# Where the bias tiles of the next region stand among the steps of a region: ten of thirteen behind column tiles, three behind row tiles

## What is computed

```python
rel  = tril(t - s)
nd   = log(|c * rel| + 1) / (log(|c * pos| + 1) + EPS)
h    = relu(nd[..., None] * W1[0] + b1)
bias = einsum('qkm,mh->qkh', h, W2) + b2
y    = x + bias
```

```python
ret = einsum('MTS,MN->NTS', y, w + eye)
ret = ret + sum_i einsum('ITS,TIM->MTS', einsum('MTS,TIM->ITS', y, qw1), qw2) + y * qdd
ret = ret + sum_i einsum('ITS,SIM->MTS', einsum('MTS,SIM->ITS', y, kw1), kw2) + y * kdd
```

## Time and profile before

| what | value |
|---|---|
| time, median of 3 runs | 895.82 us (891.65 to 903.48) |
| the profiled execution's own time | 896.75 us |
| its span, first to last instruction | 894.9 us |
| mean granted TensorE clock | 0.894 of full speed |
| busy share: PE / DVE / ACT / POOL | 78% / 54% / 44% / 57% |
| DMA packets | 148.98 MB, 166 GB/s over the span |

### The profile page before, as it was taken

One profiled execution on the slowest core, in us unless ns is written; L12 is line 12 of the kernel. 1 busy time (PEld: TensorE's weight loads), 2 busy tenths in 40 slices (PEclk: granted clock), 3 DMA queues, 4 the chain that ended last, 5 costly groups with the idle time before them and its releaser, 6 DMA issues. The chain is left out here.

```text
span 894.9 us, 28881 instructions
## 1 busy us (share of the span) xinstructions
PE 699.0 (78%) x12836; PEld 586.1 (65%) x12836; DVE 481.0 (54%) x629; ACT 395.8 (44%) x428; POOL 513.4 (57%) x463
## 2 busy tenths in 40 slices
PE   0466767986998798696699859969988896699764
PEld 0254566875887688585577657756866685589664
DVE  7667625863693595475346625653475365335412
ACT  5756536544743663563245325433543453232000
POOL 4524823734475257368558937985898588635300
PEclk9876978988998899899899979998999999799857
DMA  6578559597778979877885888589859897843905
GB/s 129 137 169 147 132 145 205 128 227 169 181 185 208 208 149 223 213 159 150 189 195 125 201 185 188 113 185 215 183 123 184 180 198 151 212 111 73 258 7 118
DMA packets 302936, 148.98 MB, mean 166 GB/s; under 512 B 31964, under 2 KB 298588, under 8 KB 302812
## 3 DMA queue, kind: packets, MB, share of 16 engines
q1 hardware_dynamic: 232928, 113.56, 57.5%
q10 hardware_dynamic: 69884, 33.58, 16.3%
HBM read 77.61 MB, written 69.47 MB: 164 GB/s over the span
## 5 line engine op out<-in xcount | busy, mean ns | idle before, releaser
L462 POOL TENSOR_TENSOR hidden<-log_table,row_scale 128x1024 f32<-128x1024 f32 x192 | 364.3, 1913 | 218.3 <-PE bias L789 210.4
L772 PEld LDWEIGHTS main<-homes,mats_b 64*64 64x64 f32 (+1 forms) x6656 | 316.9, 189 | 150.3 <-ACT homes L528 65.1
L772 PE MATMUL main<-homes,mats_b 64*64 64x104 f32 (+2 forms) x6656 | 332.5, 274 | 106.1 <-ACT homes L528 50.7
L501 ACT ACTIVATE hidden<-hidden,b_col 128x1024 f32<-128x1024 f32 x192 | 221.0, 1152 | 259.6 <-POOL hidden L462 187.6
L759 PEld LDWEIGHTS main<-homes,mats_a 64*64 64x64 f32 x4096 | 239.2, 136 | 51.3 <-issue 37.4
L759 PE MATMUL main<-homes,mats_a 64*64 64x128 f32 x4096 | 256.0, 279 | 5.2 <-POOL mats_a L439 3.5
L439 POOL TENSOR_TENSOR mats_a<-mats_in,own_block 128x256 f32<-128x256 f32 x256 | 153.6, 655 | 143.0 <-DMA mats_in<-a_mats 112.9
L651 DVE TENSOR_TENSOR homes<-main,homes 128x1024 f32<-128x1024 f32 x128 | 156.7, 1225 | 59.4 <-PE main L759 54.3
L641 DVE COPY homes<-main 128x832 f32<-128x832 f32 (+1 forms) x80 | 77.7, 971 | 192.1 <-PE main L772 189.2
L789 PE MATMUL bias<-hidden,w_blocks 64*32 64x256 f32 (+1 forms) x2048 | 120.4, 528 | 58.0 <-ACT hidden L501 46.4
L677 DVE SCALAR_TENSOR_TENSOR homes<-bias,b_col,homes 64x256 f32<-64x256 f32 x256 | 122.9, 480 | 76.7 <-DMA homes<-in_x 52.8
(11 more groups left out here) (40 smaller groups left out, 33.0 us busy)
## 6 DMA issues: line engine op xcount, KB each, us to landing
homes<-in_x SPq DMA_DIRECT2D x224, 192.0 KB, 6.2
out_mixed<-homes SPq DMA_DIRECT2D x108, 192.0 KB, 4.8
out_mixed<-homes ACTq DMA_DIRECT2D x108, 192.0 KB, 5.4
out_mixed<-homes SPq DMA_DIRECT2D x88, 128.0 KB, 3.5
out_mixed<-homes ACTq DMA_DIRECT2D x88, 128.0 KB, 3.6
homes<-in_x SPq DMA_DIRECT2D x160, 64.0 KB, 4.4
homes<-in_x SPq DMA_DIRECT2D x80, 128.0 KB, 4.5
mats_in<-a_mats SPq DMA_DIRECT2D x128, 64.0 KB
```

Of the source, the lines that this page charges most:

```text
L462: nc.gpsimd.tensor_tensor(hidden_tile(u, g).rearrange("p (j b s) -> p j b s", b=2, s=W), bass.AP(log_table, t0 - SLOTS * W * g, [[2 * TABL ...
L501: nc.scalar.activation(hidden_tile(u, g), hidden_tile(u, g), ACT.Relu, bias=b1_col[:, 0:1])\
L772: mm = pe.matmul(main[at, i % 2, j * W:j * W + REGION_TILES[k] * ROWS], b_weights(at, C * ROWS + j), y_column(k, at, C * ROWS + j), start= ...
```

## The change

`bias_step` gets another rule. For a region of 13 tiles that is followed by another of 13, bias tiles 0 to 12 stood behind steps 4, 5, 7, 9, 11, 13, 15, 17, 19, 21, 23, 25 and 27. Now they stand behind steps 1, 2, 4, 5, 7, 8, 10, 11, 13, 14, 17, 22 and 27. Steps below 16 are column tiles; the one behind step 15 stood between the last column tile and the first row tile. In region 0 they move from 4, 5, 6, 8, 9, 10, 12, 13, 14, 16, 17, 18, 20 to 1, 2, 4, 5, 7, 8, 10, 11, 13, 14, 17, 18, 20, and in region 9, which has five bias tiles of region 10, from 4, 9, 15, 21, 27 to 1, 2, 4, 5, 17. The other edits name the number of pieces loaded ahead by a function, `loads_ahead`; with these piece lists it gives 5, 3 and 2 where the code before had the same numbers, and SP's instructions stand in the same order as before.

```diff
-BIAS_FROM = 4
+BIAS_EARLY = 10
...
         def bias_step(k, T):
 
-            return BIAS_FROM + T * (COL_TILES + REGION_TILES[k] - 2 - BIAS_FROM) // (REGION_TILES[k + 1] - 1)
+            early = -(-REGION_TILES[k + 1] * BIAS_EARLY // HOME_TILES)
+            if T < early:
+                return 1 + T * 3 // 2
+            return COL_TILES + 1 + (T - early) * (REGION_TILES[k] - 3) // max(1, REGION_TILES[k + 1] - early - 1)
...
+        def loads_ahead(k):
+
+            return len(load_pieces(k)) - (REGION_TILES[k] == HOME_TILES)
...
-                while k + 1 < REGIONS and loaded[k + 1] < min(5, len(load_pieces(k + 1))):
+                while k + 1 < REGIONS and loaded[k + 1] < loads_ahead(k + 1):
```

More of the change, by code:

```diff
@@ L377, in _ @@
                 load_mats_a(v)
-            load_x(1, 4)
+            for i in range(4, loads_ahead(1)):
+                load_x(1, i)
             sp.wait_ge(tables_made, 3)
             sp.dma_start(late_scales, scale_late).then_inc(scales_out, DMA)
-            loaded = [3, 5] + [0] * (REGIONS - 2)
+            loaded = [loads_ahead(0), loads_ahead(1)] + [0] * (REGIONS - 2)
             for k in range(REGIONS):
-                while k + 1 < REGIONS and loaded[k + 1] < min(5, len(load_pieces(k + 1))):
+                while k + 1 < REGIONS and loaded[k + 1] < loads_ahead(k + 1):
                     load_x(k + 1, loaded[k + 1])
@@ L397, in _ @@
                         load_mats_a(v)
-                    if k + 1 < REGIONS and len(load_pieces(k + 1)) > 5 and T == min(6, REGION_TILES[k] - 4):
-                        load_x(k + 1, 5)
+                    if k + 1 < REGIONS and REGION_TILES[k + 1] == HOME_TILES and T == min(6, REGION_TILES[k] - 4):
+                        load_x(k + 1, loads_ahead(k + 1))
                     for i in range(len(store_pieces(k))):
-                        if T == piece_start(store_pieces(k), i + 1) - 1 - (i == 4 and k < REGIONS - 1):
+                        if T == piece_start(store_pieces(k), i + 1) - 1 - (REGION_TILES[k] == HOME_TILES and i == len(store_pieces(k)) - 1 and k < REGIONS - 1):
                             store_upper(k, i)
                     if k + 2 < REGIONS and (T in AHEAD or k == 0 and T == REGION_TILES[0] - 1) \
-                            and loaded[k + 2] < len(load_pieces(k + 2)):
+                            and loaded[k + 2] < loads_ahead(k + 2):
                         load_x(k + 2, loaded[k + 2])
```

## The result

| | before | after |
|---|---|---|
| median of four runs each, us | 893.74 (891.29 to 903.48) | 976.05 (974.71 to 982.3) |
| span of the profiled execution, us | 894.9 | 972.9 |
| mean granted clock | 0.894 | 0.867 |

What follows compares the result with a forecast made beforehand. PE's waits bound the kernel, mostly for piece 1 of x, in regions 5 and 6 for a matrix chunk. 21.8 + 12.4 + 10.2 + 15.5 - 2 = 57.9 us on 896.75 gives 955 us, range 908 to 982.

Steps and rivals of the forecast that it cites:

- the rival with more restarts: DVE and ACT may stand a third time, for piece 2, with another 2.0 us cold restart in eight regions: 971 us; chance 0.13.
- Piece 1's landing bounds a region: When piece 1 of x lands, at bias tile 1, sets the period in regions 1 to 4, 7 and 8.
- 7.2 us for three column tiles and three bias tiles, 0.8 for DVE in place of ACT: Regions 1 to 3: this extra work after piece 1's landing, less SP's 0.75 us, gives 21.8 us in all.
- The landing stays at 50 us: SP's time from row tile 1 to piece 1's landing should stay at 50 us.
- The clock: Two standstills a region, for pieces 0 and 1, but no further cold restart of 2.0 us counted.
- Region 4: 12.4 us more: 7.2 + 0.8, three dearer bias tiles at 0.53 and two ring gaps of 1.42.
- Regions 5 and 6: Bound by a matrix chunk: 8.3 us more from PE's resuming, 3.2 us back from SP, 10.2 us for both.
- Regions 7 and 8: Piece 1 decides: 13.1 us less SP's 3.2 each, less 4.3 us of slack in region 7; together 15.5 us.
- Regions 0 and 9 at nothing: Region 0 and region 9's columns put at 0; region 9's rows to save 2 us.
- The rows: Rows of regions 5 to 8 should shrink to some 28 us; only SP's 3.2 us of that counts.
- SP's row-to-landing time is issuing, not waiting: Argument against the faster rival (rows freed, 864 us, chance 0.08): SP's issuing sets when piece 1 lands.
- The signs: Region 2: DVE and ACT stand longer than 9 us for piece 1; columns of regions 5 to 8 stretch to 48 to 55 us.

Runs made afterwards that it cites:

- E1: Kernel before with bias tiles 0 and 1 behind steps 1 and 2, the other eleven unmoved; 963.72 us, ratio 1.0667 to the kernel before.
- E8: Kernel before with bias tile 0 alone moved, to behind step 1; 894.78 us, ratio 0.9939 to the kernel before.
- E9: Kernel before with bias tiles later in regions 1 to 4 (behind steps 7 to 27), tile 0 behind step 1 from region 5 on; 880.08 us, ratio 0.9735.
- E10: E9 with bias tiles later still in regions 1 to 3 (from step 8 on); 873.09 us, ratio 0.9665 to the kernel before.
- E11: Kernel before with the changed list of bias places in regions 5 to 8 alone; 938.79 us, ratio 1.0393 to the kernel before.
- E4: Changed kernel with all stores issued by ACT, none by SP; 983.99 us, ratio 1.0906 to the kernel before.
- E6: Kernel before with bias tiles later in regions 1 to 8, tile 1 behind step 8 in place of 5; 898.27 us, ratio 0.9969.

## Why the prediction was right, and where it was short

The sign and the range held, and the mechanism in all but two regions. The narrower band that had the largest chance, 930 to 970 us, did not hold: 976.05 lies above it, and near the 971 of the rival with more restarts. The total alone could not have told the two apart; the traces do. Point by point:

- *Piece 1's landing bounds a region.* Right: DVE's add follows the landing at once in every region of the changed kernel, and the place matters, as E1 beside E8 shows and, in the first half, E9 and E10 in the other direction.
- *7.2 us for three column tiles and three bias tiles, 0.8 for DVE in place of ACT.* Right: the stretch behind tile 1's add grew by 7.4, 8.5 and 8.9 us in regions 1 to 3, and 31.0 us from PE's resuming was forecast as "some 31". The three regions come to 22.4 us against 21.8; one by one they lie between 5.8 and 8.9 against 7.25, so the closeness of the sum is in part luck.
- *The landing stays at 50 us.* Right (49.8 and 49.6 in regions 2 and 3, 2.7 and 1.2 us sooner than before, where 0.75 was credited to SP).
- *The clock.* "I count no further restart" was right for the path: in region 2 one stretch at 0.53 stands behind the landing, as one at 0.50 did before. The pair of column tiles at 206.46, slowed to 4.90 us, lies ahead of the wait for piece 1, in its shadow. PE's busy time rose by 19.4 us (699.0 to 718.4) with the same instructions; the part of that in the shadow costs nothing. The other condition of that rival, a third standstill for piece 2, came in regions 3 and 7 (1.70 and 6.01 us of DVE's), where PE waited 0.19 and 0.76 us for it.
- *Region 4.* Short by 4.5 us. The stretch behind the landing grew by 12.9 us against 12.4 forecast; the rest is a landing 4 us later. E8 and E11, which leave this region's list nearly or wholly as it was, have it at 54.8 and 54.4 us as well (55.6 here, 51.6 in the trace of before), so most of that looks like scatter between executions. It wasn't measured by itself.
- *Regions 5 and 6.* This step failed: "the first bias tile starts about there", with the chunk as the bound. In the changed kernel and in E11 DVE stands for piece 1 after the chunk has come, so these regions follow the rule given for 7 and 8, 13.1 us less SP's gain. The stretch behind tile 1's add grew by 13.4 us in each. The two regions cost 18.2 us in place of 10.2. That is the largest part of the 20.1 us by which the sum was short; the trace of before had it hidden, since a wait of PE's for the chunk came earlier in the same region.
- *Regions 7 and 8.* Sized 15.5, measured 18.3. The stretches grew by 12.3 and 16.6 us, a mean of 14.5 against 13.1, and SP's gain was 5.1 to 5.5 us in place of 3.2.
- *Regions 0 and 9 at nothing.* They cost 2.9 and 1.3 us, region 9 by luck: its stretch behind tile 1's add grew by 13.6 us and the one ahead of it shrank by 12.3.
- *The rows.* Row tiles 1 to 12 of regions 4 to 8 fell from 37.1, 32.6, 38.9, 35.3 and 37.1 us to 31.5, 26.1, 28.6, 31.6 and 30.5, 32.7 us in all, where some 28 each was forecast. As argued there, the end of the rows sets nothing: of it only SP's 3 to 5.6 us a region came through.
- *"SP's row-to-landing time is issuing, not waiting".* True of both kernels, and not the whole truth: E4 shows the DMA engines close behind as the next limit.
- *The signs.* DVE stood longer than 9 us for piece 1 in region 2 (13.23), ACT did not (6.33), since POOL's hidden buffer had held it up first. The columns of regions 5 to 8 were to take 48 to 55 us; from DVE's add of the last row tile to PE's next row tile they took 61.1, 65.7, 57.3 and 56.7 (47.6, 48.7, 40.1 and 41.4 before). That is the same step again: the wait for piece 1 stands in them.
- *A slip.* 13 x 1.9 + 3 x 0.5 is 26.2 and not 27. No term of the sum uses it.

## What to carry to other kernels

Find the instruction at which an in-order engine stands for a transfer, and count what the bounding engine has still to do when that transfer lands: a step list should put as much as it can ahead of that place, and here meeting the piece three column tiles earlier cost 5.7 to 7.4 us a region in regions 1 to 3 (E1), and three later gained 3.6 to 6.4 (E6). In the second half later gained nothing, since other waits took over. Balance of work between stages came second in this kernel: most of what the rows were freed of became idle time of the next region. Before bringing a transfer forward, look at what it overtakes and at the share of the DMA engines.

## What the runs showed that was not expected

Taking half of the stores off SP's queue made the next load land hardly sooner: in region 2 it was issued 7.5 us earlier and landed 1.4 us earlier, while the DMA engines rose from some 0.85 to 0.95 busy (E4). And an early standstill for a small transfer cost nothing here, with a longer one behind it on the same engine: E8, with bias tile 0 three steps earlier, ran at 0.9939 of the kernel before (0.9904 to 0.9975).
